# Two full attentions: where a spread chunk leaves PSUM, the order of projections and spreads, and the rotation table in four loads

## The reference, cut to what matters

```python
# L1: all keys
q, k, v = proj(wq, bq), proj(wk, bk), proj(wv, bv)
attn = softmax(einsum('bhqd,bhkd->bhqk', q, k) * scale)
out = einsum('bhqk,bhkd->bhqd', attn, v) @ wo + bo
# L3: rotated q and k, a bias by distance, causal
q = q * cos + rotate_half(q) * sin        # k the same
att = (einsum('bhid,bhjd->bhij', q, k) + bias[None]) * (1.0 / sqrt(D))
att = where(causal, att, -inf)
y = einsum('bhij,bhjd->bhid', softmax(att), v) @ Wp + bp
```

## Time and profile before

| | us |
|---|---|
| time, median of 3 runs (lowest, highest) | 3872.7 (3872.69, 3880.21) |
| the profiled execution's own time | 3874.09 |
| its span, first to last instruction | 3872.3 |
| PE busy in the span | 3352.8 (87%) |
| DVE busy | 2715.2 (70%) |
| ACT busy | 1863.9 (48%) |
| POOL busy | 973.4 (25%) |
| granted TensorE clock, mean share of full speed | 0.915 |

### The profile page before, as it was taken

How to read it: one execution, slowest core, us unless ns; L and a number is a source line. 1 busy time by engine, 2 the same in 40 slices (tenths; PEclk the granted TensorE clock), 3 DMA queues, 4 the chain that set the end, 5 groups by cost and what they waited for, 6 DMA issues and landing times.

```text
span 3872.3 us, 55774 instructions
## 1 busy us (share of the span) xinstructions
PE 3352.8 (87%) x21901; PEld 1712.6 (44%) x21909; DVE 2715.2 (70%) x5772; ACT 1863.9 (48%) x3334; POOL 973.4 (25%) x772
## 2 busy tenths in 40 slices
PE   2679875699989999999979998988998888899899
PEld 2322223465652333333246666656775322323576
DVE  7787868787758999999477774464434786875433
ACT  1232221377755777777757773323222365667321
POOL 0235542377730000000076670000201110211100
PEclk8879877799988999999989998989999699999899
DMA  0000000211100000000031110001100000000100
GB/s 20 9 1 1 0 1 0 67 31 37 31 10 1 1 1 1 1 1 1 1 82 27 34 27 23 6 23 42 50 1 28 1 1 1 1 1 1 45 1 12
DMA packets 48255, 60.16 MB, mean 16 GB/s; under 512 B 9268, under 2 KB 34232, under 8 KB 47608
## 3 DMA queue, kind: packets, MB, share of 16 engines
q1 hardware_dynamic: 47992, 56.59, 5.3%
HBM read 39.22 MB, written 1.10 MB: 10 GB/s over the span
## 4 chain that ended last, share of the span: by engine, by line


## 5 line engine op out<-in xcount | busy, mean ns | idle before, releaser
L142 PE MATMUL ps<-AR 32*128 32x512 bf16 (+8 forms) x16848 | 2153.5, 434 | 162.4 <-DVE AR L114 35.2
L131 ACT ACTIVATE AR<-ps 128x1024 f32<-128x1024 f32 (+6 forms) x1768 | 1277.1, 762 | 1112.6 <-PE ps L142 838.6
L142 PEld LDWEIGHTS ps<-AR 128*128 128x128 f32 (+5 forms) x16848 | 1028.1, 152 | 1318.6 <-DVE AR L125 399.6
L125 DVE TENSOR_REDUCE AR<-ps 128x1 f32<-128x512 f32 (+1 forms) x1424 | 935.9, 708 | 83.2 <-PE ps L142 82.3
L114 POOL TENSOR_TENSOR AR<-AR 128x512 f32<-128x512 f32 (+4 forms) x422 | 551.9, 1320 | 825.1 <-ACT AR L131 564.3
L131 ACT ACTIVATE AR<-ps,AR 128x128 f32<-128x128 f32 (+1 forms) x764 | 402.5, 544 | 391.7 <-PE ps L142 363.6
L114 POOL TENSOR_TENSOR rs<-rs,halves 128x4 f32<-128x4 f32 x68 | 71.1, 1046 | 1849.2 <-DVE rs L118 1780.1
L142 PE MATMUL ps<-XT,AR 128*128 128x512 f32 x896 | 428.3, 613 | 3.2 <-DMA AR<-in_L3f_w 3.1
L114 DVE TENSOR_TENSOR AR<-ps,AR 128x512 f32<-128x512 f32 (+3 forms) x626 | 299.8, 527 | 127.7 <-PE ps L142 96.4
L122 DVE SCALAR_TENSOR_TENSOR X<-ps,AR,X 128x128 f32<-128x128 f32 x512 | 143.7, 344 | 345.0 <-PE ps L142 344.7
L150 PE MATMUL ps<-C,AR 128*128 128x128 f32 x1593 | 249.3, 294 | 139.7 <-ACT AR L131 61.4
(11 more groups left out here) (84 smaller groups left out, 1849.5 us busy)
## 6 DMA issues: line engine op xcount, KB each, us to landing
AR<-AR SPq DMA_DIRECT2D x124, 128.0 KB, 2.3
AR<-in_c_rot SPq DMA_DIRECT2D x64, 128.0 KB, 2.3
AR<-in_L3f_w SPq DMA_DIRECT2D x32, 256.0 KB, 5.9
AR<-in_L2f_w SPq DMA_DIRECT2D x32, 128.0 KB, 2.7
AR<-scr_bias SPq DMA_DIRECT2D x32, 128.0 KB, 3.2
WR<-in_c_rot SPq DMA_DIRECT2D x1, 2048.0 KB, 9.3
WR<-in_L_ffn_wqkv SPq DMA_DIRECT2D x2, 768.0 KB
AR<-in_L_ffn_wqkv SPq DMA_DIRECT2D x2, 768.0 KB
```

What stands on the lines that cost most here:

```text
L125: return self.do(lambda e: e.tensor_reduce(o, a, AXX, op, negate=neg, apply_absolute_value=mag), *w)
L131: return self.do(lambda e: e.activation(o, a, f, bias=bias, scale=scale, accum_out=acc), *w)
L142: last = e.matmul(o, l, r, start=a, stop=z, skip_group_check=True)
```

## The change

A spread now has one reader of its bank: ACT copies the bank as f32 to a new SBUF tile `RAW` (three buffers, as many as `HI` has now), and the bank is free after that. From `RAW`, ACT makes the bf16 `HI`, POOL makes `QK` (`tensor_scalar` with per-partition operands), and DVE makes the low part. A buffer is free again when both the low part and POOL's operation are done, and the readers of `QK` and `MQK` wait for both. At the start the projections of a chunk are appended ahead of the spreads of the chunk before. In the main loop `flush` comes after `step_products`. The rotation table is loaded in four parts of 512 columns, each with a semaphore of its own, the first ahead of the weights, and a rotation waits for its part alone.

```diff
+    trot = []
+
+    def load_rotation(c):
+        cols = slice(512 * c, 512 * c + 512)
+        trot.append((g.d_r, g.d_h, g.d_b, g.d_scr)[c].load(S, ROT[:, :, cols], I["c_rot8"][:, :, cols]))
+    if causal:
+        g.wr.at = 0
+        ROT = g.wr.f32(2, 2048)
+        load_rotation(0)
     for k in range(len(names)):
         g.d_w.load(S, W[:, k, :], I[pre + names[k]])
     g.d_w.load(S, bqk, I[pre + "bqk"])
     g.d_w.load(S, MK, I["c_rep"])
     tw = g.d_w.load(S, bvb, I[pre + "bvo"])
+    if causal:
+        for c in range(1, 4):
+            load_rotation(c)
...
-    HI = ar.bf16(4, 512)
+    HI = ar.bf16(3, 512)
+    RAW = ar.f32(3, 512)
...
-        g.wr.at = 0
-        ROT = g.wr.f32(2, 2048)
-        trot = g.d_r.load(S, ROT, I["c_rot8"])
...
-        g.free[b] = t = V.stt(RC[:, k, cols], g.bank[b], bqk[:, k:k + 1], ROT[:, 0, cols], ALU.add, ALU.mult, t, trot)
+        g.free[b] = t = V.stt(RC[:, k, cols], g.bank[b], bqk[:, k:k + 1], ROT[:, 0, cols], ALU.add, ALU.mult, t, trot[c])
...
     def spread(gr, c, k, b):
-        s, x = gr % slots, nhi[0] % 4
+        s, x = gr % slots, nhi[0] % 3
         nhi[0] += 1
         cols = slice(512 * c, 512 * c + 512)
         t = P.mm([(g.bank[b], REP[:, gr, :], RC[:, k, cols], True, True)], g.free[b], trc[c, k], trep)
+        traw = g.free[b] = A.act(RAW[:, x, :], g.bank[b], ACT.Copy, t, hif[x])
+        thi = A.act(HI[:, x, :], RAW[:, x, :], ACT.Copy, traw)
         if k:
-            A.act(QK[:, 1, s, cols], g.bank[b], ACT.Identity, t, tw, skf[s], scale=MK[:, 0:1], bias=MK[:, 3:4])
+            tqk = G.ts(QK[:, 1, s, cols], RAW[:, x, :], MK[:, 0:1], MK[:, 3:4], ALU.mult, ALU.add, traw, tw, skf[s])
         else:
-            A.act(QK[:, 0, s, cols], g.bank[b], ACT.Copy, t, tw, skf[s], scale=MK[:, 0:1])
-        t = A.act(HI[:, x, :], g.bank[b], ACT.Copy, hif[x])
-        return gr, c, k, b, x, t
-
-    def spread_low(gr, c, k, b, x, t):
+            tqk = G.ts(QK[:, 0, s, cols], RAW[:, x, :], MK[:, 0:1], None, ALU.mult, None, traw, tw, skf[s])
+        return gr, c, k, x, thi, tqk
+
+    def spread_low(gr, c, k, x, thi, tqk):
         s = gr % slots
-        g.free[b] = hif[x] = tsp[gr, c, k] = V.stt(MQK[:, k, s, 512 * c:512 * c + 512], HI[:, x, :], MK[:, 1 + k:2 + k],
-                                                   g.bank[b], ALU.mult, ALU.add, t)
+        t = V.stt(MQK[:, k, s, 512 * c:512 * c + 512], HI[:, x, :], MK[:, 1 + k:2 + k], RAW[:, x, :], ALU.mult, ALU.add,
+                  thi, tw)
+        hif[x] = tsp[gr, c, k] = [t, tqk]
...
     for c in range(5):
+        if c < 4:
+            for k in (1, 0):
+                compact(c, k)
         if c >= 1:
             for k in (1, 0):
                 later.append(spread(0, c - 1, k, 5 + k))
-        if c < 4:
-            for k in (1, 0):
-                compact(c, k)
         flush()
...
     for j, (n, kt) in enumerate(steps):
+        step_products(n, kt, target(p + area[j]))
         flush()
-        step_products(n, kt, target(p + area[j]))
```

More of the change, by code:

```diff
@@ L1215, in attn8 @@
     tsp = {}
-    hif = [None] * 4
+    hif = [None] * 3
     nhi = [0]
```

## The result

The changed kernel takes 3851.7 us (median of 4 runs, 3844.6 to 3855.3) against 3872.7: a ratio of 0.9941 with a 95% interval of [0.9919, 0.9962]. By the 0.2% that the prediction set, that is faster. The profiled execution took 3855.3 us, the longest of the four, and 18.8 less than that of before.

The account below looks back on a forecast made before the run. DVE was taken to bound the non-causal spread stretch, waits and PE holes the causal start and loop. -11.5 - 1.2 - 6 + 4 = -14.7 us from 3874.1 gave 3859.4, as median 3858 us; range 3842 to 3870.

Parts of the forecast that it names:

- The waits: Causal attention: DVE's first rotation waits 8.18 us for the table; in the loop DVE waits 32.1 us for ACT's copy.
- the collision: Non-causal spread stretch: DVE's low part with two SBUF operands meets Pool's SBUF operation every other round, +5 us.
- Causal start: Start of the causal attention: earlier table and projections ahead of spreads bring the first maximum forward, -11.5 us (-7 to -14).
- Non-causal start: Start of the non-causal attention: PE's work per chunk 3.84 us against 4.18, three times 0.34, -1.2 us (0 to -2.5).
- The causal loop: Causal main loop: bank returned about 1.3 us earlier, low part behind the step's reduces, -6 us (0 to -14).
- The most that this gives is the 14.5 us of idle PE: Causal loop: the gain is capped by PE's idle time in 24 windows of 3.8 us; somewhat less than half taken.
- The spread stretch: Non-causal stretch making the 24 spreads of head groups 1 to 3: collision +5 with -1.1, +4 us (-1 to +11).
- The saving of 1.1 for reading SBUF: Non-causal spread stretch: the low part reading SBUF alone takes 0.687 us against 0.73, 24 x 0.05 = -1.1 us.
- The blocking in full: Non-causal spread stretch: by the skill's rule the operation issued second blocks fully, costing 24 x 0.30 = 7 us.
- The clock didn't hold in the causal start: Rival, chance 0.13: the causal stretch at 0.51 clock runs at 2.4 GHz, some 12 us more go, 3846 us.
- Pool wasn't the bound: Rival, chance 0.09: Pool's operation sets the spread stretch's round, slower from 3.0 us on; at 3.4 us, 3891 us.
- the collision eats the gain: Rival, chance 0.16: Pool's operation takes as long as an addition and the loop's holes stay, 3870 us median, no change.

Follow-up runs that it names:

- the second measurement: The changed kernel, unedited, measured again beside the kernel before: 3843.5 us, ratio 0.9927 [0.9914, 0.9940].
- the changed kernel's first profile: Profiled execution from the changed kernel's first comparison with the kernel before: 3855.3 us, its loop 599.4 us.

## Why the prediction was right, and where it wasn't

The waits and the collision that the prediction named are the ones that the runs show, but three of the four terms were off in size, and the sum came out by luck: predicted -14.7, measured in the profiled execution -7.9 - 1.2 - 12.5 + 7.0 = -14.6. Of the other 4 us of its gain, 3.0 lie in stages without an edit and 1.0 in the non-causal steady part, where no spread is left. In the second measurement the same kernel gained 29 us by the medians, twice the forecast.

**Causal start, -11.5 predicted, -7.9 in this execution.** The steps hold: no wait for the table, and a chunk of 5.15 us (5.42 predicted). What fell short was the place of PE's start. The last small load was issued 4.66 us after the stage's start, against 3.70 before, so the slot ahead of it cost 0.96 us and not 0.47; it then took 4.06 us to land, and the first projections ran partly at 1.2 GHz. In executions without the late landing the first maximum stood at 31.3 to 33.4 us (predicted 30.9, and 32.4 with all collisions), 10.5 to 12.6 before that of the old kernel. Both edits carry it: the parts 3 to 5 us, the order 6 to 8 (39.7 without).

**Non-causal start, -1.2 predicted, -1.2 measured.** The agreement is partly luck. A chunk fell by 0.74 us, not by 0.34: the prediction added up two durations that overlap. Three times 0.74 would be 2.2, and in this execution PE's first projection began 0.7 us later. In the profiles of kernels with this start unedited the first reduce comes at 27.4 to 29.3 us, and with the old order at 29.2, so what the order brings to the whole stage isn't shown.

**The causal loop, -6 predicted, -12.5 measured: the term that was mis-sized.** The step that failed is "The most that this gives is the 14.5 us of idle PE". As an estimate of idle time it was good: PE's idle time fell by 4.1 us in all, by 7.3 behind the first 54.5 us. But the term took PE's busy time as unchanged, and that fell by 8.5, of which 5.2 behind the first 54.5 us. The size differs between executions too: in the eleven profiles with low parts last the loop takes 588.3 to 599.9 us, so the gain is 12 to 24 us, mostly beyond the term's bound of 14.

The idle part is itself a difference: the order is worth 8.5 to 10.7 us of idle time (74.5 and 76.8 with low parts first, 66.0 and 66.1 last), while the new chain without the order costs 4 to 6.5 against before's 70.3. Why it costs that wasn't tried; ACT's split now stands behind its copy. Of the busy time: the three profiled loops with low parts first, before's among them, have 538.7 to 541.7 us, all eleven with low parts last 522.0 to 533.4, for the same products. So the busy time goes with the order, but why stays open. By the rows the granted clock can be only a part of it. In the stretch shown it is 0.97, against 0.95 and 0.92 with low parts first; but over the whole loop it is 0.88 in all three with low parts first and 0.87 to 0.90 in the eleven, and the changed kernel's first profile has 0.88 like before's, with 8.5 us less busy time.

**The spread stretch, +4 predicted, +7.0 measured.** The collision is right in kind and size: the 23 low parts ahead of the last took 24.6 - 3.45 = 21.2 us, against 23 x 0.734 = 16.9, so +4.3 where +5 was taken. Pool's operation on the keys takes 0.76 us (0.75 assumed); that on the queries takes 1.56, which no term had, and costs no more. The alternation fits the cause that the prediction gave: a low part held up shifts the next round past its collision. The saving of 1.1 for reading SBUF isn't there: a free low part takes 0.74 from SBUF too. The step that was missed is a move: before, `tb` ran on Pool at 1150.05, ahead of the spreads; now it stands behind the spreads' operations, and it holds the last low part for 2.7 us. Where it doesn't strike, the stretch of 49.2 and 49.5 us is 3.2 and 3.5 longer than before's, near the +4.

The Trainium skill (SBUF — State Buffer, "Who interferes with whom") has the rule that the runs bear out: contention needs two SBUF inputs on DVE's side (1.15 us against 0.76 with one from PSUM), and the one issued second waits. The blocking in full, which the prediction took from there, isn't what the rows show: behind an operation of 0.76 us, a low part that begins 0.14 us later loses 0.42 us, not 0.62.

**The rivals and the range.** The clock didn't hold in the causal start: over the 54.5 us from the first maximum it was 0.62, against 0.51. What it rose gave almost nothing, since PE idles 8.9 us there instead of 5.7. Pool wasn't the bound: its operations take up to 1.6 us, and a round 2.0 in the mean. That the collision eats the gain fails on the loop. Two sums of the prediction don't come out: with Pool at 1.34 us its own steps give 24 x 0.52 = 12.5 for the collision, not 11, and the terms all at their bounds give 3841 to 3877, not 3845 to 3866. Neither decides the forecast.

## What to carry to other kernels

An engine that waits at the head of a step for a chain on another engine holds up everything queued behind it: look for work of that step that can be issued first, and for the buffer that has to come free early to allow it. Before an operation moves to another engine's queue, list what was queued there and what it now stands behind, and which operand pairs then meet in SBUF: leaving one operand in PSUM took the collision away, and the stretch was as long as before (46.0 us). A term worked out from idle time alone misses what happens to the busy time, and the time of one execution can agree with a sum whose terms are off.

## What the runs showed of the hardware that was not expected

- GpSimd's multiply by a per-partition scalar, 128x512 f32, takes 1.55 to 1.58 us where VectorE doesn't read two SBUF operands beside it; the same with an addition behind it takes 0.69 to 0.77. The longer form holds VectorE up no longer than the shorter: a low part that began 0.48 us behind it lost nothing, and one that began 0.15 us behind it took 1.08 us instead of 0.74.
- A load of 128 KB issued behind some 900 KB took 2.1 to 2.7 us to land in eight profiles, and 3.77 and 4.06 in two.
- The same 16 projections took 7.13 us at a granted clock of 1.00, 8.98 at 0.79 and 9.66 at 0.74, in kernels with the same instructions in this place.
